# Shared up products of a sparse feed-forward layer, two token tiles at a time with stationary weights

## The reference

```python
xp = einsum('ntd,dh->nth', x, Wx) + b
next_h = tanh(xp_t + prev_h @ Wh)                      # 1024 steps
shared = silu(h @ shared_w1.T) @ shared_w2.T           # 256 -> 1024 -> 256
gate_logits = h @ gate_w.T                             # 8 experts
top_k_gates, top_k_idx = top_k(gate_logits, 2); softmax of the two
expert_out = einsum('teh,edh->ted', silu(einsum('td,ehd->teh', h, experts_w1)), experts_w2)
return x + shared + sum over the two chosen experts of gate * expert_out
```

## Time and profile before

| | us |
|---|---|
| median of 3 runs | 382.85 |
| lowest, highest | 382.18, 384.53 |
| the profiled execution, its own time | 382.14 |
| its span in the profile | 380.4 |

### The profile page before, as it was taken

The page is one execution under the profiler, slowest core; times in us unless marked ns, Lnnn a source line. Parts: engine busy times, 40 slices in busy tenths (PEclk is TensorE's granted clock), DMA queues, the critical chain, the costliest instruction groups (busy, mean ns, idle before and its releaser), DMA issues.

```text
span 380.4 us, 8835 instructions
## 1 busy us (share of the span) xinstructions
PE 357.3 (94%) x2440; PEld 254.6 (67%) x2441; DVE 197.6 (52%) x422; ACT 237.1 (62%) x461; POOL 109.6 (29%) x101
## 2 busy tenths in 40 slices
PE   8979999999999499797999999999999999999991
PEld 7758899965666366574666666666666666666671
DVE  0599889978698688873432233332333323233310
ACT  3876788887784557663566555666555666555630
POOL 0100001000068888800032422233322333322342
PEclk9998999999999699999999999999999999999997
DMA  7999999607788999999899999998888988888982
GB/s 217 432 429 425 430 400 334 219 16 106 148 186 179 230 232 219 272 200 191 145 178 137 163 160 152 153 163 146 156 143 147 155 148 159 149 149 146 166 140 30
DMA packets 167068, 75.58 MB, mean 199 GB/s; under 512 B 149248, under 2 KB 163712, under 8 KB 165760
## 3 DMA queue, kind: packets, MB, share of 16 engines
q1 hardware_dynamic: 155952, 62.45, 69.3%
q0 software_dynamic: 6864, 9.11, 16.2%
q10 hardware_dynamic: 4224, 3.67, 3.8%
HBM read 23.68 MB, written 16.53 MB: 106 GB/s over the span
## 4 chain that ended last, share of the span: by engine, by line
PE 70%; DMA 11%; SPq 4%; DVE 4%; ACT 4%; issue 3%; POOL 0%; ACTq 0%; POOLq 0%; DVEq 0%
PE py L1224 27%; PE z L1108 25%; PE z L1124 8%; DMA space<-recurrence_w 6%; PE z L1071 4%; PE z L1039 3%; DMA sorted_rows<-space 3%; SPq L387 2%; ACT space L874 1%; DVE w_slots L598 1%; PE px L1082 1%; SPq L360 1%; PE py L1039 1%; DMA out<-space 1%; DMA space<-x_cols 1%
## 5 line engine op out<-in xcount | busy, mean ns | idle before, releaser
L1224 PE MATMUL py<-w_slots,space 128*128 (+1 forms) x1272 | 150.4, 275 | 11.2 <-DMA space<-recurrence_w 10.8
L1224 PEld LDWEIGHTS py<-w_slots,space 128*128 128x128 f16 x1272 | 124.8, 99 | 39.8 <-issue 10.8
L1108 PE MATMUL z<-w_slots,x 128*128 (+1 forms) x636 | 145.7, 379 | 0.0
L1108 PEld LDWEIGHTS z<-w_slots,x 128*128 128x128 f16 x636 | 62.1, 98 | 64.4 <-issue 0.6
L505 POOL DMA_INDIRECT out<-space x37 | 58.0, 1567 | 155.6 <-DMA out<-space 66.0
L944 ACT ACTIVATE space<-z,tile_scales 128x512 f32<-128x512 f32 x105 | 70.9, 676 | 37.7 <-PE z L1108 35.2
L654 DVE SCALAR_TENSOR_TENSOR recurrence_w<-space,tile_scales,recurrence_w 128x512 f16<-128x512 f32 x54 | 40.0, 751 | 79.8 <-ACT recurrence_w L951 69.5
L654 DVE SCALAR_TENSOR_TENSOR space<-space,tile_scales 128x512 f16<-128x512 f32 x52 | 38.5, 750 | 58.1 <-ACT space L951 44.2
L951 ACT ACTIVATE recurrence_w<-space,tile_scales 128x512 f16<-128x512 f32 x54 | 39.0, 722 | 22.7 <-DMA space<-recurrence_w 13.9
L480 POOL DMA_INDIRECT sorted_rows<-space x32 | 38.8, 1213 | 46.9 <-issue 45.2
L598 DVE SCALAR_TENSOR_TENSOR w_slots<-w_slots,w_scale 128x1024 f16<-128x1024 f32 x36 | 46.2, 1284 | 1.9 <-ACT w_slots L991 0.7
(11 more groups left out here) (122 smaller groups left out, 166.5 us busy)
## 6 DMA issues: line engine op xcount, KB each, us to landing
w_slots<-weights SPq DMA_DIRECT2D x8, 2048.0 KB, 30.8
sorted_rows<-pad_row SPq DMA_DIRECT2D x1, 5070.0 KB, 58.5
w_slots<-weights SPq DMA_DIRECT2D x2, 1024.0 KB, 9.7
out<-space ACTq DMA_DIRECT2D x8, 256.0 KB, 3.6
space<-x_cols SPq DMA_DIRECT2D x3, 512.0 KB, 9.3
space<-x_rows ACTq DMA_DIRECT2D x6, 256.0 KB
space<-recurrence_w SPq DMA_TRANSPOSE x55, 2.7
space<-space SPq DMA_TRANSPOSE x52
```

Source lines behind the costliest of these rows:

```text
L1108: last = nc.tensor.matmul(Z[u % 2][h][:], x16[:, u, x_part, k], weight(f, k * HID + h * BANK, BANK, part), start=k == 0 and x_part == 0 an ...
L1224: last = nc.tensor.matmul(PY[p][:, 0:D], hiddenT[:, p, low, q], weight(f, MATRIX + q * D, D, part), start=q == 0 and not low and part == 0 ...
```

## The change

- The up products of the shared tiles are computed for two tiles together with the weights stationary and the states of both tiles moving (256 columns). A half-step g stands for half of the hidden units of the pair (g even: the first 512, g odd: the last). The result has hidden units on the partitions and is what `down` needs, so the shared tiles' transposes go. The down product of a tile now needs both half-steps of its pair.
- `hidden`, the parts of the activations and their waits are buffered by pair; the buffers of the parts are `hidden_rows` and the space of `hiddenT` in turn. The first transpose of a sorted tile waits for down(15).
- TensorE's order: up 0 to 3, down 0, down 1, prefix sums, then up g+2, down g for g = 2 to 13, then the gate (`split_ok`, `tiles_ok`), up 16, down 14, down 15, up 17, then as before.
- The states of step j and, in the same place, its token-major row with the four numbers of `meta` are `states_rows[:, j + 1]`, 264 numbers wide. The ring `hr`, the copies of `meta` on GpSimd and their waits go.
- `shared_rows`, `states_low` and `turn_rows` work on two tiles at once. The stores move from ScalarE's queue to SP's.
- `find_last(0)` moves behind the first silu; `route_slots` and `route_rows` both stand at g = 3.

```diff
@@ sizes, buffers
-SPACE = 2 * K * NTOK + 2 * HID - 512
+SPACE = 2 * K * NTOK + 2 * HID - 768
-ROWS_AT = {1: (2,), 2: (3, 4), 3: (5,), 4: (6,), 5: (7, 8), 6: (9, 10), 7: (11,), 8: (12, 13), 9: (14,), 10: (15,)}
-STATES_AT = {0: (2, 3), 1: (4,), 2: (5, 6), **{t - 4: (t,) for t in range(7, TILES)}}
+OUTPUTS_AT = {3: (0, 1), **{g: (g - AHEAD,) for g in range(4, TILES)}}
-        states = sb("states", [P, K, L + 1, COLS])
+        states_rows = sb("states_rows", [P, L + 1, ROW_PITCH])
+        states = states_rows[:, :, 0:K * COLS].rearrange("p j (k n) -> p j k n", k=K)
+        meta = states_rows[:, 1:L + 1, D:ROW]
+        pair_parts = [[v.rearrange("p s n -> p (s n)") for v in hidden_rows],
+                      [turned_parts[:, s * 2 * HID:(s + 1) * 2 * HID] for s in range(2)]]
@@ SP
-                if part == 0 and not (isinstance(g, int) and g < AHEAD):
-                    sp.wait_ge(down_mm, g - 1)
+                if part == 0:
+                    sp.wait_ge(down_mm, TILES if isinstance(g, int) and g == TILES else g - 1)
+            def turn_rows(j):
+
+                sp.wait_ge(x_lo_ok, j + 1)
+                for t in (2 * j, 2 * j + 1):
+                    sp.dma_start_transpose(rows16[:, t + 1, 0:2 * D].rearrange("p (a n) -> p a n", n=P),
+                                           x16[:, t % RING].rearrange("p a k n -> p (a k n)")).then_inc(row_in[t % RING], 16)
+
+            def store(j):
+                v = j % 2
+                sp.wait_ge(y_ok, 2 * j + 2)
+                sp.dma_start(out_pairs[j], ys[:, 2 * v:2 * v + 2]).then_inc(stored[v], 16)
+                if j + 2 < PAIRS:
+                    sp.dma_start(x_res[:, 2 * v:2 * v + 2], x_pairs[j + 2]).then_inc(x_res_in[v], 16)
+
+            sp.wait_ge(h_hi_ok, 1)
+            turn_rows(0)
+            turn_rows(1)
+            turn_rows(2)
+            turn_rows(3)
+            for j in range(PAIRS - 4):
+                store(j)
+                turn_rows(j + 4)
+            store(PAIRS - 4)
+            for k in range(TOP):
+                sp.wait_ge(sorted_ok[k], 16 * TILES)
+            load(0, 0)
+            load(1, 1)
+            store(PAIRS - 3)
+            load_meta(0, 2 * RING)
+            load(2, 2)
+            load(3, 3)
+            store(PAIRS - 2)
             for t in range(RING):
                 turn(TILES + t, t % 2)
+                if t == 0:
+                    store(PAIRS - 1)
                 load(t + RING, t)
@@ GpSimd
-                if t >= SORT_RING:
-                    pool.wait_ge(row_copied, t - SORT_RING + 1)
                 waited(row_in[t % RING], 16 * (t // RING + 1))
                 for k in range(TOP):
                     nc.gpsimd.indirect_dma_start(
                         out=sorted_slots, out_offset=bass.IndirectOffsetOnAxis(slots_u[:, t, k:k + 1], 0),
-                        in_=hr[:, u, 0:ROW], in_offset=None).then_inc(sorted_ok[u], 16)
+                        in_=states_rows[:, t + 1, 0:ROW], in_offset=None).then_inc(sorted_ok[k], 16)
-                    waited(sorted_ok[v % SORT_RING], 16 * TOP * (v // SORT_RING + 1))
-                    nc.gpsimd.tensor_copy(hr[:, v % SORT_RING, D:ROW], meta[:, v + SORT_RING]).then_inc(row_copied, 1)
@@ VectorE
             route_gap()
+            pair_low(0, 0)
+            pair_low(0, 1)
+            pair_low(1, 0)
+            pair_low(1, 1)
             states_low(2)
-            hidden_low(0, 0, None, 0)
...
             route_best()
-            hidden_low(1, 1, None, 1)
+            pair_low(2, 0)
+            pair_low(2, 1)
             route_choice()
-            states_low(4)
             route_gates()
+            for g in range(3, TILES):
+                pair_low(g, 0)
+                pair_low(g, 1)
+                if g % 2:
+                    if g + 3 < TILES:
+                        states_low((g + 3) // 2)
+                for t in OUTPUTS_AT[g]:
+                    shared_y(t)
+                if g == 3:
                     route_slots()
                     route_rows()
@@ ScalarE
+            shared_rows(0, x_hi_ok)
             step_pair(z_mm, h_ok, r, L // 2 - 1, 1, find_at, chunks)
-            find_last(0)
+            shared_rows(1, x_hi_ok)
...
             silu_first(hidden_ok)
+            find_last(0)
+            def silu_half(g, p, h):
+                act.wait_ge(up_mm, g * HALVES + (h + 1))
+                if not (isinstance(g, int) and g < 2):
+                    act.wait_ge(h_lo_ok, (g - 2) * HALVES + (h + 1))
...
+            def pair_half(g, h):
+
+                if g or h:
+                    silu_half(g, g % 2, h)
+                act.wait_ge(hidden_ok, g * HALVES + (h + 1))
+                if h == 0 and g % 2 == 0 and g >= 4:
+                    act.wait_ge(down_mm, g - 2)
+                high_half(g, g % 2, h, pair_part(g, h, 0))
@@ TensorE
+            def pair_up_half(g, h, done):
+
+                u, p = g // 2 * 2 % RING, g % 2
+                for b in range(2):
+                    q = p * (Q // 2) + h * 2 + b
+                    for k in range(K):
+                        for x_part, part in ((0, 0), (1, 0), (0, 1)):
+                            last = nc.tensor.matmul(Z[p][h][:, b * 2 * P:(b + 1) * 2 * P],
+                                                    weight(SHARED, k * HID + q * P, P, part), x16[:, u:u + 2, x_part, k],
+                                                    start=k == 0 and x_part == 0 and part == 0,
+                                                    stop=k == K - 1 and part == 1)
+                last.then_inc(done, 1)
+            def pair_down(g):
+                if g >= 2:
+                    pe.wait_ge(y_ok, g - 1)
+                for low in range(2):
+                    pe.wait_ge((h_hi_ok, h_lo_ok)[low], (g // 2 + 1) * 2 * HALVES)
+                    for q in range(Q):
+                        start = (2 * q + g % 2) * P
...
+            for g in range(2, 4):
+                pair_up(g)
+            pair_down(0)
+            pair_down(1)
+            prefix_sums()
+            for g in range(2, TILES - AHEAD):
+                pair_up(g + AHEAD)
+                pair_down(g)
+            pe.wait_ge(split_ok, FFNS * WIDES)
+            pe.wait_ge(tiles_ok, 1)
+            up(TILES, 0, expert(0), 16)
+            pair_down(TILES - 2)
+            pair_down(TILES - 1)
+            up(TILES + 1, 1, expert(1), 16)
```

More of the change, by code:

```diff
@@ L55 @@
 ROW_PITCH = ROW + 4
-SORT_RING = 6
 BANK = 512
@@ L1081, in router @@
                     for k in range(K):
-                        last = nc.tensor.matmul(PX[:, t * E:(t + 1) * E], states[:, k, t + 1], gate_sb[:, k],
+                        last = nc.tensor.matmul(PX[:, t * E:(t + 1) * E], states[:, t + 1, k], gate_sb[:, k],
                                                 start=k == 0, stop=k == K - 1)
```

276 lines of the change are left out of this document (108 added, 168 removed).

## The result

The changed kernel took 370.61 us (median of 4, 368.65 to 372.66) against 383.15 us before: ratio 0.970, interval 0.9655 to 0.9745. The profiled execution took 370.42 us, its span is 368.3. That was one job on the chip (the kernels of one job run on the same chip, in turn with the kernel before). The same file gave 392.16 us in a second job (ratio 1.023, so slower than the kernel before) and 370.39 in a third: the gain of 3% is that of two jobs out of three.

What follows compares the result with a forecast made beforehand. TensorE was taken to bound the kernel, with 14.6 us lost in the shared-tile stretch. Gains of 8.6 up to up(16) and 2.5 behind it, less 0.8 for small waits, took 382.14 to 371.8 us; range 368.0 to 377.3.

Steps and rivals of the forecast that it cites:

- the wait that was to set the start of up(16): Ahead of up(16), TensorE waits for the first expert load behind the sort, starting at about 162.1, 3.0 us late.
- 14.6 us lost to the transposes, and what becomes late next: Shared tiles, TensorE: waits on activation transposes cost 14.6 us, the bound of the gain; the sort is late next.
- The shared up product: Per shared tile, 24 matmuls of 256 columns replace 12 of 512: 2.62 for 2.59 us, 0.5 us more.
- Down(2) waits 0.7 to 0.9 for y(0): At down(2), TensorE arrives at 98.9 while VectorE's y(0) ends at 99.5: 0.7 to 0.9 us lost with the restart.
- The sort: GpSimd's 32 scatters start at 106.2, take 49.3 us; load lands 162.0, up(16) starts 8.6 us earlier than before.
- The port, named as the reason why the mean may rise: VectorE operations holding the port shared with GpSimd may lengthen scatters; all 32 at 0.1 more would be 3.2 us.
- Behind up(16), 2.5 us: From up(16) to up(19), 18.1 us for 15.6 of work: the 2.5 lost on tile 14's transposes goes.
- 0.8 us of small waits: Shared steps: VectorE's margin is only 0.5 to 2 us from 110 to 150, so 0.8 us of waits is allowed.
- The sum: Whole kernel: 8.6 + 2.5 - 0.8 = 10.3 us off the profiled 382.14, giving 371.8; chance 0.60.
- the other rivals: VectorE/ScalarE pace 375.8 (0.12); sort's pace worse 390.0 (0.04); transposes not cause 379 to 382 (0.05); narrow ups some 414 (0.01).
- The first rival: The sort keeps up, with the median scatter of 1.07 us: 369.4 us, chance 0.18.
- the wait of 1 to 3 us ahead of up(16): Sign that the forecast is right: a single TensorE wait of 1 to 3 us there, released by a load of sorted rows.

Runs made afterwards that it cites:

- the loop kernel: The changed kernel with the twelve middle steps of the shared stage as a hardware loop run three times, in place of written-out code; 371.88 us, ratio 0.973.

## Why the prediction was right, and where it was off

The size of the gain came out. It came out of a right account of the work and of the transposes, and of some luck: the wait that was to set the start of up(16) is not there in the kernel as changed, an idle time that nobody forecast stands in its place, and in job 2 the same file lay 15 us above the stated range.

- **14.6 us lost to the transposes, and what becomes late next.** Right in that no wait on a transposed activation is left in the shared stage. The prediction gave the gain to the transposes alone; the experiment without them shows that it also takes the four buffers. The sort as the next limit is half right: the loop kernel waits 1.21 us for it at up(16), but the changed kernel does not, the data being there some 1.0 us earlier by the landing time of 2.7. With the scatters begun 9.6 us later the load goes out at 164.71 in place of 157.16 and the kernel takes 8.9 us more; but there the stall had made TensorE as late, so that kernel does not show the sort as the limit by itself.
- **The shared up product.** Right: 2.62, also with the moving operand in two runs of 128 columns.
- **Down(2) waits 0.7 to 0.9 for y(0).** Wrong, there is no such wait. In its place stands the gap of 1.97 us in the branches, of which the prediction had nothing. The first up came 0.47 us early, as the last steps of the recurrence already did (77.23 for 77.70); which part of the change does this was not looked into. Together TensorE reaches up(16) at 160.86, where the prediction had 159.1 without any wait and 160.0 with that for y(0).
- **The sort.** Start 104.32, not 106.2; but 1285 ns a scatter, not 1213, so it took 154.60 + 0.96 - 104.32 = 51.2 us, not 49.3, and ended at 155.56 where 155.5 was written: two errors of 1.9 us that cancel. What was mis-sized is the landing: 4.0 us from a scatter's start in the prediction, where the load went out 157.16 - 154.60 = 2.6 us after the last scatter's start. That puts the load 1.0 us earlier than the 158.2 of the prediction. Its own landing was taken too long as well, 3.7 us for the 2.7 that the loop kernel shows. With both, the sort was ready 2 us before the 162.0 of the prediction, and up(16) starts when TensorE's work lets it.
- **The port, named as the reason why the mean may rise.** Borne out. VectorE's low part of a weight (L604) and the scatter beside it:

```profile
127.18 1.28 DVE L604 SCALAR_TENSOR_TENSOR w_slots<-w_slots,w_scale 128x1024 f16<-128x1024 f32 x1
```
```profile
127.57 1.73 POOL L490 DMA_INDIRECT sorted_rows<-states_rows,space  x1 [0.30 <-issue]
```

The scatter ends 0.84 us after VectorE's operation does. Every scatter of the trace that begins while an L604 runs ends 0.83 to 0.92 us behind it (14 of them), whether that makes it 1.02 or 1.97 long; those that begin at most 0.5 us ahead of one take 0.96 to 1.02. In the kernel whose late low parts have one input in PSUM the second scatter, well before the stall of that job, shows the difference by itself:

```profile
105.90 1.28 DVE L605 SCALAR_TENSOR_TENSOR w_slots<-w_slots,w_scale,px 128x1024 f16<-128x1024 f32 x1
```
```profile
106.29 0.96 POOL L490 DMA_INDIRECT sorted_rows<-states_rows,space  x1 [0.30 <-issue]
```

It ends 0.07 us behind VectorE's operation and takes 0.96; in the changed kernel the second scatter, at 106.08 beside the same L604 at 105.69, took 1.72. By line, in the changed kernel in job 1, in the one with an input in PSUM, and in the changed kernel in job 2 (minimum, median, maximum):

```profile
L490 POOL DMA_INDIRECT sorted_rows<-states_rows,space x32: 960/1036/1965, 104.3 to 154.6; - x32
```
```profile
L490 POOL DMA_INDIRECT sorted_rows<-states_rows,space x32: 957/963/1462, 104.5 to 166.3; - x32
```
```profile
L490 POOL DMA_INDIRECT sorted_rows<-states_rows,space x32: 956/960/1934, 106.0 to 171.6; - x32
```

With the input in PSUM none over 1.46 is left, where job 2 without the edit still has 1.93. The lower median shows nothing by itself: job 2 has it too, without the edit, since the stall frees VectorE. The Trainium skill ("SBUF — State Buffer", Who interferes with whom) has the rule that an operation with two SBUF inputs holds the port that VectorE and GpSimd share for its length, and by that rule the trace agrees: the same operation, of the same duration, with one input elsewhere does not delay the scatter. The mean is 1026 in that job against 1093 for the changed kernel in job 2. What the edit would do to the time without a stall was not seen.
- **Behind up(16), 2.5 us.** Right to the tenth: 176.49 - 160.86 = 15.63, exactly the work.
- **0.8 us of small waits.** There are none in the steps.
- **The sum.** 371.8 for 370.42. Up(16) came 1.2 us earlier than forecast, and the 0.8 of small waits is not there; against that, 0.6 of the 12.3 gained up to 176.49 does not reach the time (the span is 12.1 shorter, the executions differ by 11.7). No wait on lows or highs set the pace, and the narrow ups cost nothing, so the other rivals did not come in this job. The first rival, the sort keeping up (369.4), is the nearer description of how it looks; its reason, the median scatter, is not what happened (1285 ns, above the old mean). Of the signs named, the wait of 1 to 3 us ahead of up(16) did not show in the changed kernel, only in the loop.
- **What no case held:** that the change can put the kernel at a second level, 392 us, by a stall that goes with a run of close scatters and whose cause is open. It was faster in two jobs and slower in one, with variants of it at the higher level in two more.

## What to carry to other kernels

When a copy between two stages is taken away, count the buffers again: the copy was also what set its source free, and without it the same ring can cost more than the copy did. Where an engine is freed of waits, look not only at which limit comes next but at what those waits may have kept apart: here the kernel before has at most five close scatters in a row in its trace, and the changed kernel has seven and more. And run a change in more than one job: four executions within about 1% said nothing about a level 21 us away. Where a stall has no releaser in the timeline, look at the queues too: here the packets of an instruction queue spoke against the first theory without a further run.

## What was not expected of the hardware

- TensorE nearly idle for about 20 us, between matmuls that have no wait between them in the program, and with no packet of q8 moving: 32 matmuls in 20 us (120 to 140 us, changed kernel, job 2). The unedited kernel had it in all four executions of one job by their times, and in none of two others; it began 6.6 us after the first of a run of indirect DMA issues, most of them 1.26 to 1.33 us apart, and ended 3.5 us after the last.
- TensorE's branches over bodies that are not entered: 1.43 to 1.98 us for two in nine traces, 1.38 for one in one trace, nothing in the kernel before; with two, the profile names another engine as the releaser.
- A one-column f32 matmul takes 213 ns for each of its two passes at the start of the kernel (20.48 us for 96, at full granted clock), about twice what a 256-column f16 matmul takes later (109 ns). Each pass has a weight load of its own, and these were busy for 20.6 us of the same stretch; which of the two sets the time is not shown.
